# Two-layer graph attention, one core: the loop of the engines runs four groups in a turn in place of one

## The chip, the cores and the metric

The kernel runs on one core of one Trainium2 chip. The metric is the time of one execution on the device in microseconds (us), the median of three runs. Both kernels compute the same outputs.

## What is computed

128 graphs of 128 nodes with 384 features pass two residual blocks. Each block normalises the rows, applies a relu, projects to q, k and v with 384x384 weights, and attends with 12 heads of 32. The first block masks the scores where the adjacency is zero and adds 0.1 times the adjacency; the second adds the adjacency as a bias, treats rows that are all zero, and has an output projection.

```python
h = relu(layernorm(x))
q, k, v = heads(h @ W0q + b0q), heads(h @ W0k + b0k), heads(h @ W0v + b0v)
s = where(adj > 0, q @ k.T / sqrt(32) + beta * adj, -9e15)
x = x + join(softmax(s) @ v)
h = relu(layernorm(x))
q, k, v = heads(h @ W1q.T), heads(h @ W1k.T), heads(h @ W1v.T + b1v)
s = q @ k.T * 384 ** -0.5 + adj          # rows that are all 0 give 0
x = x + join(softmax(s) @ v) @ W1o.T + b1o
```

## The kernel before, in words

Four graphs make a group, so there are 32 groups. A unit is one layer of one group, 64 units in all, and the units are interleaved (`unit`, `loop_unit`, lines 83 to 94): layer 0 of the next group runs ahead of layer 1 of this one. A phase (`Phase`, line 97) is a slice of time in which several units are at different stages: the tail of one unit, the attention of the next, the projections of the one after it, the scores that are already looked up for that one, and the layer norm of a fourth. A phase has twelve slots (4 graphs by 3 chunks of four heads) with some places in each, and the constants of lines 39 to 73 say in which slot and place each step is issued.

Each engine has its own stream of instructions, written out by its own `phase` function, and `run_phases` (line 160) lays the phases out for it: the phases of `before()` written out one after the other, then a hardware loop (`Fori`, line 163) whose body holds the two phases of `inside(i)`, for i from 2 to 29, then the seven phases of `after()` written out. The first two phases of `after()` are the same phases as a turn of the loop. All five engines, SyncE (SP, which issues every DMA), GpSimd (POOL), ScalarE (ACT), VectorE (DVE) and TensorE (PE), run such a loop. They are tied together by semaphores alone: a wait compares a semaphore with a count that is worked out from the unit's number, `u.n`, which within the loop is a register expression of i.

The lines that the prediction speaks of:

- PE: projections L839 (`project`), scores L852, transposes of the probabilities L862, probabilities times values L879, output projection L913 to L917, and the transposes of the inverse sums L899 (`turn_inverse`), which wait for DVE's `inv_wide` L702.
- DVE: biased scores L647 behind a small memset L621 (`carry`) that carries waits, the inverse sums L689 to L702, and `take_v` L724, the last thing that a phase issues on DVE.
- ACT: exponentials L539, the copy of the turned probabilities L564, the high part of the output L578 (`high_o`), which PE's L913 waits for, and the first instructions that a turn issues on ACT.
- All: L163, the `Fori` itself, with its addition, its compare and branch, and the first register operation of a turn.

Of the kernel before, what the change touches and what calls it, by code (L numbers as in the profile page):

```python
# [90 lines left out]
def loop_unit(i, off):  # L91
    if off % 2:
        return Unit(i * 2 + off, 0, i + (off + 1) // 2, i + (off - 1) // 2, 1)
    return Unit(i * 2 + off, 1, i + (off // 2 - 1), i + off // 2, 0)
# [25 lines left out]


FIRST_LOOP, LAST_LOOP = 2, GROUPS - 3


def before():
    u = unit
    return [
        Phase(norm=u(0)),
        Phase(project=u(0), norm=u(1), look=u(0), bias=0),
        Phase(attend=u(0), project=u(1), look=u(1), bias=1),  # L130
        Phase(tail=u(0), norm=u(2)),
        Phase(attend=u(1), project=u(2), norm=u(3), look=u(2), bias=2, keep=0),
        Phase(attend=u(2), project=u(3), norm=u(4), look=u(3), tail=u(1)),
    ]


def inside(i):
    return [
        Phase(tail=loop_unit(i, -2), attend=loop_unit(i, -1), project=loop_unit(i, 0),
              look=loop_unit(i, 0), norm=loop_unit(i, 1), bias=i + 1, keep=i - 1),  # L140
        Phase(tail=loop_unit(i, -1), attend=loop_unit(i, 0), project=loop_unit(i, 1),
              look=loop_unit(i, 1), norm=loop_unit(i, 2)),
    ]


def after():
    u, n = unit, UNITS
    return [
        Phase(tail=u(n - 6), attend=u(n - 5), project=u(n - 4), look=u(n - 4), norm=u(n - 3),
              bias=GROUPS - 1, keep=GROUPS - 3),  # L150
        Phase(tail=u(n - 5), attend=u(n - 4), project=u(n - 3), look=u(n - 3), norm=u(n - 2)),
        Phase(tail=u(n - 4), attend=u(n - 3), project=u(n - 2), look=u(n - 2), keep=GROUPS - 2),
        Phase(tail=u(n - 3), norm=u(n - 1)),
        Phase(attend=u(n - 2), project=u(n - 1), look=u(n - 1)),
        Phase(tail=u(n - 2), attend=u(n - 1), keep=GROUPS - 1),
        Phase(tail=u(n - 1)),
    ]


def run_phases(eng, phase, first=0):  # L160
    for p in before()[first:]:
        phase(p)
    with eng.Fori(FIRST_LOOP, LAST_LOOP + 1) as i:  # L163
        for p in inside(i):
            phase(p)
    for p in after():
        phase(p)

# [37 lines left out]
def build(nc, x, adj, w0q, b0q, w0k, b0k, w0v, b0v, beta, w1q, w1k, w1v, b1v, w1o, b1o, out):  # L206
    weights = (w0q, w0k, w0v, w1q, w1k, w1v, w1o)
    w_scale = (QK0_SCALE, QK0_SCALE, W_SCALE, W_SCALE, W_SCALE, W_SCALE, W_SCALE)
    with ExitStack() as ctx:
# [143 lines left out]
        def _(sp):  # L353
# [30 lines left out]
            def phase(p):  # L384
                for s in range(SLOTS):
# [43 lines left out]
                    if s == 11 and p.look is not None and isinstance(p.look.n, int) and p.look.n == UNITS - 1:  # L429
                        sp.wait_ge(neg_ready, p.look.n * SLOTS)  # L430
                        sp.dma_start(adj1[:, :, :], adj_groups[p.look.group]).then_inc(adj1_in, 16)

            run_phases(sp, phase)
            for b in range(GROUP):
                sp.wait_ge(stored[b], 16 * GROUPS)

        @block.gpsimd
        def _(pool):
# [65 lines left out]
            def phase(p):  # L504
                for s in range(SLOTS):
# [14 lines left out]
                    if p.keep is not None and s in KEEP_SLOTS:  # L520
                        add_out_bias(p.keep, KEEP_SLOTS.index(s))

            run_phases(pool, phase)

        @block.scalar
        def _(act):
# [86 lines left out]
            high_weights(3, WEIGHTS)  # L613
            act.wait_ge(cols_ready, 3)
            run_phases(act, phase, 1)

        @block.vector
# [362 lines left out]
```

## Time and profile before

| | |
|---|---|
| median of 3 runs | 2375.24 us (2373.09 to 2375.53) |
| profiled execution | 2368.63 us |
| its span, first to last instruction | 2366.8 us |
| PE busy | 2208.3 us, 93% |
| ACT busy | 2058.5 us, 87% |
| DVE busy | 1834.5 us, 78% |
| POOL busy | 1521.9 us, 64% |
| DMA queue of the program | 66.4% of 16 engines |

The profile is of one execution. Busy shares are unions of instruction times; register, branch, semaphore and DMA-issuing instructions aren't counted as busy and are shown with a "q" behind the engine's name. "issue" as the releaser of a wait means that the engine waited for nothing that the profile shows. PEclk is the granted share of TensorE's clock: 1.00 is 2.4 GHz and 0.50 is 1.2 GHz. PEld is the weight load, which overlaps PE.

### The profile page before, as it was taken

The numbers are of one execution on the slowest core, as the hardware profiler recorded it, in microseconds if no ns is written. First come the engines' busy times: TensorE is split into PE (matmuls) and PEld (weight loads), VectorE is DVE, ScalarE is ACT, GpSimd is POOL, SyncE is SP. The second block draws the span as 40 slices with busy tenths as digits, with TensorE's granted clock in tenths as the row PEclk, the third lists the DMA queues.
The fourth block names the chain that finished last, engine by engine and source line by source line (L and its number), as shares of the span: only waits on it lengthen the run. The fifth ranks groups of instructions, "written<-read, shape, count | busy, mean of one in ns | idle before, by whom it ended". The sixth has DMA issues, their size and how long they took to land.

```text
span 2366.8 us, 77473 instructions
## 1 busy us (share of the span) xinstructions
PE 2208.3 (93%) x19968; PEld 1441.5 (61%) x19968; DVE 1834.5 (78%) x10186; ACT 2058.5 (87%) x7816; POOL 1521.9 (64%) x2439
## 2 busy tenths in 40 slices
PE   3699999999999999999999999999999999999977
PEld 1366666666666666666666666666666666666645
DVE  4478778787788887778788778787878787788856
ACT  3599998898898898898898898998998998899967
POOL 3276667676666676666676666676666676677645
PEclk9799999999999999999999999999999999999989
DMA  7587675686676676675776676776666776666731
GB/s 176 109 133 128 130 135 122 129 148 115 127 136 122 132 148 114 127 135 117 138 139 120 126 131 122 141 137 119 129 130 122 142 134 121 130 128 134 119 85 46
DMA packets 461103, 300.48 MB, mean 127 GB/s; under 512 B 228432, under 2 KB 460880, under 8 KB 460880
## 3 DMA queue, kind: packets, MB, share of 16 engines
q1 hardware_dynamic: 460880, 298.45, 66.4%
q14 instruction: 198, 1.62, 0.3%
q8 instruction: 25, 0.41, 0.1%
HBM read 71.83 MB, written 25.17 MB: 41 GB/s over the span
## 4 chain that ended last, share of the span: by engine, by line
PE 72%; DVE 14%; issue 8%; POOL 1%; DMA 1%; ACT 1%; DVEq 1%; SPq 1%; POOLq 0%; ACTq 0%
PE job_bank L839 43%; PE pt_bank L862 11%; PE score_bank L852 6%; PE o_bank L879 6%; DVE neg L647 4%; PE inv_bank L899 2%; PE post_bank L891 2%; DVE v L724 2%; DVE inv_wide L702 1%; DVE row_sum L691 1%; DVE live L697 1%; DVE off_zero L693 1%; DVE neg_max L647 1%; PE post_bank L917 1%; PE post_bank L913 1%
## 5 line engine op out<-in xcount | busy, mean ns | idle before, releaser
L539 ACT ACTIVATE probs<-neg,neg_max 128x128 f32<-128x128 f32 x3072 | 1189.7, 394 | 99.8 <-DVE neg_max L647 99.8
L839 PE MATMUL job_bank<-h,w_hi 128*128 128x512 f16 x2304 | 746.4, 391 | 73.9 <-DMA h<-h_rows 41.2
L539 ACT ACTIVATION_READ_ACCUMULATOR probs<-neg,neg_max 128x1 f32 x3072 | 595.4, 194 | 0.0
L564 ACT ACTIVATE probs_t<-pt_bank 128x512 f32<-128x512 f32 x768 | 450.5, 587 | 49.4 <-PE pt_bank L862 45.3
L862 PE MATMUL pt_bank<-ident,probs 128*128 128x128 f32 x3072 | 473.5, 278 | 9.4 <-ACT probs_t L564 8.4
L839 PE MATMUL job_bank<-h,w_lo 128*128 128x512 f16 x1152 | 448.7, 389 | 0.0
L862 PEld LDWEIGHTS pt_bank<-ident,probs 128*128 128x128 f32 x3072 | 375.5, 144 | 97.0 <-issue 17.8
L478 POOL TENSOR_TENSOR pair_sum<-neg 128x256 f32<-128x256 f32 x384 | 279.8, 729 | 217.8 <-DVE neg_max L647 207.9
L839 PE MATMUL job_bank<-w_hi,h 128*128 128x384 f16 x1536 | 413.5, 327 | 0.2 <-DVE part_lo L710 0.2
L839 PEld LDWEIGHTS job_bank<-h,w_hi 128*128 128x128 f16 x2304 | 224.7, 100 | 280.6 <-issue 91.8
L647 DVE CUSTOM_DVE_ANT_0 neg<-score_bank,bias 128x128 f32<-128x128 f32 x1536 | 353.6, 286 | 45.0 <-issue 42.5
L647 DVE CUSTOM_DVE_ANT_0 neg<-score_bank,adj 128x128 f32<-128x128 f32 x1536 | 353.4, 286 | 18.9 <-issue 18.9
L852 PEld LDWEIGHTS score_bank<-stack 96*128 96x128 f16 x3072 | 235.5, 98 | 130.0 <-issue 14.6
L852 PE MATMUL score_bank<-stack 96*128 96x128 f16 x3072 | 303.9, 222 | 3.5 <-DMA stack<-part_lo 2.7
L453 POOL TENSOR_TENSOR rstd<-shift_var,minus_half 128x1 f32<-128x1 f32 x256 | 140.7, 550 | 203.7 <-DVE shift_var L680 201.7
L647 DVE DVE_READ_ACCUMULATOR2_ANT neg_max<- 128x1 f32 x3072 | 254.4, 83 | 0.0
L469 POOL TENSOR_TENSOR h_rows<-h_rows 128x384 f16<-128x384 f32 x256 | 239.2, 934 | 21.4
L839 PE MATMUL job_bank<-w_lo,h 128*128 128x384 f16 x768 | 251.0, 327 | 0.0
L492 POOL TENSOR_TENSOR x_mid<-x_res,o_rows 128x384 f32<-128x384 f32 x128 | 127.9, 999 | 172.8 <-DVE o_rows L753 153.0
L879 PE MATMUL o_bank<-probs_t,v 128*32 128x128 f32 x6144 | 221.3, 277 | 1.4 <-ACT probs_t L564 1.4
L715 DVE SCALAR_TENSOR_TENSOR part_lo<-job_bank,part_hi 128x512 f16<-128x512 f32 x192 | 132.6, 691 | 108.4 <-ACT part_hi L555 107.8
L484 POOL TENSOR_TENSOR four_sum<-pair_sum 128x128 f32<-128x128 f32 x384 | 176.4, 459 | 31.0
(57 smaller groups left out, 3516.1 us busy)
## 6 DMA issues: line engine op xcount, KB each, us to landing
stack<-part_hi SPq DMA_DIRECT2D x768, 128.0 KB, 3.4
stack<-part_lo SPq DMA_DIRECT2D x384, 128.0 KB, 3.9
x_norm<-in_x SPq DMA_DIRECT2D x32, 768.0 KB, 6.2
x_res<-in_x SPq DMA_DIRECT2D x32, 768.0 KB, 5.1
out_x<-result SPq DMA_DIRECT2D x128, 192.0 KB, 3.3
adj<-in_adj SPq DMA_DIRECT2D x64, 256.0 KB, 3.1
h<-h_rows SPq DMA_TRANSPOSE x256, 3.9
stack<-in_L_gnn_Wq SPq DMA_DIRECT2D x2, 576.0 KB, 7.3
```

Source lines behind the costliest of these rows:

```text
L453: pool.tensor_tensor(rstd[:, b % 2:b % 2 + 1], shift_var[:, b % 2, 1:2], minus_half[:, :], ALU.pow).then_inc(rstd_done, 1)
L469: pool.tensor_tensor(h_rows[b % 2][:, 1, :], h_rows32[:, :], h_rows[b % 2][:, 0, :], ALU.subtract).then_inc(h_rows_ready, 1)
L478: pool.tensor_tensor(pair_sum[:, :, :], neg[c % 2][:, :, 0:NODES // 2], neg[c % 2][:, :, NODES // 2:NODES], ALU.add).then_inc(pair_sum_don ...
L484: pool.tensor_tensor(four_sum[b % 2][:, first:first + HC, :], pair_sum[:, :, 0:NODES // 4], pair_sum[:, :, NODES // 4:NODES // 2], ALU.add ...
L539: last = act.activation(probs[c % 2][:, h, :], neg[c % 2][:, h, :], ACT.Exp, bias=neg_max[:, b, first + h:first + h + 1], scale=-1.0, accu ...
L564: act.activation(probs_t[b % 2][:, first:first + HC, :].rearrange("p h q -> p (h q)"), pt_bank[:, :], ACT.Copy).then_inc(probs_t_ready, 1)
L647: last = dve.tensor_tensor_reduce(out=neg[c % 2][:, h, :], in0=score_bank[c % 2][:, P * h:P * (h + 1)], in1=bias, scale=(-1.0 / SCORE0 if ...
L715: last = dve.scalar_tensor_tensor(part_lo[t][:, c, :], job_bank[j % 2][:, :], scale, part_hi[t][:, c, :], ALU.mult, ALU.subtract)
L839: last = pe.matmul(to, stationary, moving, start=(m == 0), stop=(m == MATMULS - 1))
L852: last = pe.matmul(score_bank[c % 2][:, P * h:P * (h + 1)], q[0:3 * HEAD, c % KC, h, nodes], k[0:3 * HEAD, c % KC, h, nodes], start=True, ...
L862: last = pe.transpose(pt_bank[:, P * h:P * (h + 1)], probs[c % 2][:, h, :], ident[:, :])
L879: last = pe.matmul(o_bank[d:d + HEAD, f:f + P], v32[u.parity][:, b, HEAD * h:HEAD * (h + 1)], probs_t[b % 2][:, h, :], start=True, stop=True)
```

## The change

The loop takes steps of four, and its body holds the eight phases of `inside(i)` to `inside(i + 3)` one after the other. Its bounds become 2 and 27, so it has 7 turns in place of 28 and covers the same i from 2 to 29. The phases, the order of the instructions within them and the semaphores stay; the counts that the waits compare with are worked out from i + k in place of i. The code ahead of the loop and behind it stays.

```diff
 FIRST_LOOP, LAST_LOOP = 2, GROUPS - 3
+TURN = 4
...
 def run_phases(eng, phase, first=0):
     for p in before()[first:]:
         phase(p)
-    with eng.Fori(FIRST_LOOP, LAST_LOOP + 1) as i:
-        for p in inside(i):
-            phase(p)
+
+    with eng.Fori(FIRST_LOOP, LAST_LOOP + 2 - TURN, TURN) as i:
+        for k in range(TURN):
+            for p in inside(i + k):
+                phase(p)
     for p in after():
         phase(p)
```

## Rows read from the trace of the kernel before

**Rows 1.** The chain of work that ended last: start us, us, what.

```profile
251.00 2.48 issue
...
320.98 2.93 issue
...
2102.27 2.44 issue
```

**Rows 2.** Instructions of line 163 between 240 and 260 us, the first turn's end.

```profile
L163 SPq COMPARE_BRANCH  x1: 63/63/63, 243.6 to 243.6; - x1
L163 SPq FUSED_REGOPS  x1: 51/51/51, 243.9 to 243.9; - x1
L163 PEldq COMPARE_BRANCH  x1: 247/247/247, 248.3 to 248.3; - x1
L163 PEldq FUSED_REGOPS  x1: 59/59/59, 248.6 to 248.6; - x1
L163 ACTq COMPARE_BRANCH  x1: 45/45/45, 249.9 to 249.9; - x1
L163 ACTq FUSED_REGOPS  x1: 65/65/65, 250.2 to 250.2; - x1
L163 DVEq COMPARE_BRANCH  x1: 68/68/68, 250.4 to 250.4; - x1
L163 DVEq FUSED_REGOPS  x1: 85/85/85, 253.5 to 253.5; - x1
```

**Rows 3.** Waits of PE, DVE and ACT from 251.00 to 2172.21 us: total, times, longest.

```profile
PE inv_bank L899 <- DVE inv_wide L702: 59.7, 27, 2.6
...
DVE carrier_v L621 <- issue: 78.8, 27, 3.3
...
ACT probs L539 <- DVE neg_max L647: 89.4, 81, 2.3
```

**Rows 4.** Windows: start:end length, busy us (count) of each engine, PEclk, DMA share, GB/s.

```profile
2172.21:2239.55 67.34, 67.04 (x626) 44.49 (x625) 56.34 (x321) 63.50 (x245) 47.58 (x76) 1.00 0.72 123
183.59:251.00 67.41, 67.25 (x626) 44.23 (x625) 56.80 (x319) 63.75 (x246) 47.50 (x76) 1.00 0.74 139
392.74:464.25 71.51, 69.06 (x626) 45.22 (x625) 56.94 (x319) 64.11 (x245) 47.49 (x76) 0.98 0.69 129
678.80:748.58 69.78, 67.63 (x626) 44.32 (x626) 56.78 (x319) 63.87 (x245) 47.49 (x76) 1.00 0.70 132
251.00:2172.21 1921.21, 1856.71 (x16849) 1214.92 (x16848) 1536.99 (x8588) 1729.08 (x6589) 1282.55 (x2052) 0.98 0.69 130
```

**Rows 5.** A stretch of 3.4 us some 7 us behind a turn's start, same columns.

```profile
471.30:474.70 3.40, 3.40 (x15) 2.04 (x14) 2.80 (x18) 2.58 (x10) 2.35 (x5) 0.50 0.00 0
```

**Rows 6.** DMA queues from 251.00 to 2172.21 us: packets, MB, share of 16 engines.

```profile
q14 instruction: 161, 1.32, 0.3%
```

**Rows 7.** DMA queues from 2172.21 to 2239.55 us, same columns.

```profile
q8 instruction: 5, 0.08, 0.6%
q14 instruction: 8, 0.07, 0.4%
```

**Rows 8.** Timeline around the first turn's end: DVE, ACT and PE in turn.

```profile
249.98 1.01 DVE L724 SCALAR_TENSOR_TENSOR v<-job_bank,bv_rows 128x384 f32<-128x384 f32 x2
253.81 0.06 DVE L621 MEMSET carrier_v<- 128x1 f32 x1 [2.81 <-issue]
...
250.47 0.51 ACT L578 ACTIVATE o_hi<-o_norm 128x384 f16<-128x384 f32 x1
...
254.82 0.40 ACT L539 ACTIVATE probs<-neg,neg_max 128x128 f32<-128x128 f32 x1 [1.82 <-DVE neg_max L647]
...
251.93 0.32 PE L913 MATMUL post_bank<-w_hi,o_hi 128*128 128x384 f16 x1
...
253.92 0.86 PE L879 MATMUL o_bank<-probs_t,v 128*32 128x128 f32 x24
256.90 0.55 PE L899 MATMUL inv_bank<-ident,inv_wide 128*128 128x128 f32 x3 [2.11 <-DVE inv_wide L702]
```

## The prediction

> **What bounds the kernel now.** I read the chain of waits first. It runs through PE's matmuls nearly everywhere, and once in each turn of the loop it has a piece called "issue", of 2.4 to 2.9 us, in which nothing that the profile shows was waited for [rows 1]. The pieces begin exactly where DVE's last `take_v` of a turn ends, so they sit on the loop's back edge. The instructions of the loop's own line say what happens there. SP, PE, ACT and POOL go from their compare-and-branch to the first register operation of the next turn in some 0.3 us; DVE takes 3.1 us (250.4 to 253.5) [rows 2]. So DVE's sequencer is without instructions for about 3 us at each of the 27 taken back edges. The waits confirm it: DVE's carrier stood idle 78.8 us in 27 pieces for "issue", and PE waited 59.7 us in 27 pieces, 2.21 us each, for DVE's `inv_wide` [rows 3]. PE is the bound and passes each of these waits on.
>
> The windows tell what a turn costs with and without the edge. The last two phases written out ahead of the loop and the first two behind it do the work of a turn with no taken branch in between: 67.41 and 67.34 us, with PE busy 67.25 and 67.04 us of it at clock 1.00. The loop's turn at 392.74 us took 71.51 us at a mean clock of 0.98, that at 678.80 us 69.78 us at 1.00, and all 27 together 1921.21 us, 71.16 each [rows 4]. So the mean back edge costs 71.16 - 67.38 = 3.78 us: 2.2 us of PE's wait, and some 1.5 us because in most turns the granted clock goes to 0.50 (1.2 GHz) for 3.4 us once PE has been idle [rows 5]. The turn without that drop cost 2.4 us, those with it some 4.1.
>
> **Fetching.** The loop moved 161 packets on the queue named instruction, q14, and none on q8; the written-out stretch behind it moved both [rows 6, 7]. 161 packets in 27 turns are six a turn. I read this as DVE fetching its body anew each turn, and stalling on the first packet alone, while PE's 1251 matmuls and loads in a turn (626 and 625) stay on the chip. ACT issues 245 counted instructions a turn and does not stall, DVE 319 and does [rows 2, 4]; the limit of what these two keep lies between, control instructions aside.
>
> The Trainium skill, page "Runtime: NRT & Kernel Launch", section Instruction fetch mechanics, says the same in figures: 512 instructions kept for most engines and 2048 for PE, and a stall where a taken branch leaves the window that is held. That four-fold bodies of ACT and PE miss would follow from it; no run here shows PE missing. The trace agrees in that DVE misses and PE doesn't, though DVE's 319 counted instructions alone would fit.
>
> **The change, part by part.**
>
> *21 back edges go.* Seven turns have 6 taken edges, in place of 27. At 3.78 us each, 21 give 79.4 us. What is late next in their place: nothing much, as the two written-out stretches show, where PE is busy 99.6% of the time and ACT 63.5 us of 67.3 [rows 4]. ACT is the next bound at about 94%, POOL and DVE have 20 and 11 us to spare.
>
> *Code in one piece costs more fetching.* The body now streams through PE's store too. The written-out stretch has just this: 5 packets on q8 and 8 on q14 in 67 us, and it ran at 67.34 us, so I price streaming at nothing, covered by the sequencers' lead over their engines [rows 4, 7]. If that cover failed, each missed packet would cost up to DVE's 3 us.
>
> *Waits with i + k.* The register operations in front of the waits may get one more addition. They run on the sequencers, which are ahead. The loop's turn at full clock took 69.78 us, and 69.78 less PE's wait of 2.2 is 67.6, against 67.38 with constant counts [rows 3, 4]: at most 0.2 us a group for register operations altogether. One more of them: between 0 and 0.2 us a group, 0 to 6 us in 28 groups; I take nothing, and keep 6 for the range.
>
> *The six edges left get dearer.* ACT's body grows to 980 counted instructions, POOL's to 304, PE's to some 5000, SP's likewise four-fold. ACT passes the size at which DVE misses by far, so ACT misses with DVE; PE, POOL and SP perhaps. The bounds: nothing more than now (3.8 us), if all misses lie beside DVE's; and one more 3.1 us after another for ACT and PE, with a second clock drop of 1.7, so 3.8 + 3.1 + 3.1 + 1.7 = 11.7 us. What the first turn's end says [rows 8]: ACT branches at 249.9 [rows 2] and would go on at 253.0. Its `o_hi`, now at 250.47, would come at 253.3 and end at 253.8. PE, which now starts L913 at 251.93, would wait 1.9 us there, then has the 2.85 us of work that now ends at 254.78, so is ready at 256.65, before `inv_wide` releases L899 at 256.90. Behind that, ACT's four exponentials (1.6 us) come after `o_hi` in place of before DVE's stall, so the copy L564 and with it PE's L879 come near 256.5, and L899 at about 257.3: 0.4 us more. ACT's next exponentials start at 256.4 rather than 254.82, 1.6 us late on an engine with 6% to spare. So between 0.4 and 1.6 us more, I take 1.2: 5.0 us an edge. PE's own miss would start at its branch, 248.3, 2.1 us ahead of DVE's; if it is as long as DVE's it ends at 251.4, before the place of L913 (251.93), and what it delays falls inside the wait that PE has there anyway. POOL has nothing to do behind its branch, and SP branches 7 us ahead of DVE with only loads due far later.
>
> **Sum.** Against the profiled execution of 2368.63 us (span 2366.8): 27 edges at 3.78 go, -102.1; 6 at 5.0 come, +30.0; net -72.1, so 2296.5 us. The median of the runs lies 6.6 us above the profiled execution; carried over, 2303 us.
>
> **The rivals.**
>
> *A. The misses add up at the six edges, or straight code is a little slower than the two stretches promise.* Five engines ask for code within 8 us, and each restart is followed by waiting for the next engine's. At 11.7 us an edge that is 6 x 6.7 = 40 us more: 2343. For it: ACT has little slack, and two stretches of 67 us are a thin base for 28 groups. Against: the misses start within 2.2 us of each other, so they overlap. A slip of 1 us a group in the long body would also give 28 us, 2331.
>
> *B. The six edges stay as cheap as now, or cheaper,* because PE's idle time doesn't always bring the half clock: at 2.4 to 3.8 us each, 7 to 16 us less than forecast, 2287 to 2296. For it: all stalls lie side by side by the working above.
>
> *C. Slower: the long body's fetching isn't hidden.* The place is each engine's crossing into code that isn't on the chip, now that PE, ACT and POOL stream as well as DVE. DVE's 3.1 us is the price. A turn of four groups has some 8 x 4 = 32 packets on q14 and 20 on q8 by the written-out stretch. The gain to be eaten is 72 us, 10.3 a turn; from four exposed misses a turn beyond the edge it is gone. With eight, 7 x 24.8 = 174 us more, 2477. Against it: DVE crosses into fetched code some five times a turn already and stalls once, and the stretches at both ends show none.
>
> *D. DVE's 3 us isn't fetching but a fixed price of something else in the loop's head,* so that it returns every two phases. The first phases behind the loop show no such stall [rows 4], so this has almost nothing; it would give 2375.
>
> **How the numbers follow.** Forecast, 5 us an edge and covered streaming: 0.62. A: 0.14. B: 0.17. C: 0.05. D: 0.02. The predicted time is the forecast's, 2303. The range goes from B's 2290 to where A is half in, 2328 (an edge of about 9 us, or 0.9 us a group); C, D and the rest of A are left out. 0.2%, 5 us, is about what a measurement of this kernel can tell from no change. Faster by more takes the forecast, A, B and a mild C: 0.95. Same: D, 0.02. Slower: C, 0.03.
>
> **What would show it.** In the new profile, "issue" waits of DVE's carrier should fall from 27 pieces to 6; the instructions of line 163 should show 6 taken branches with 3 us behind them on DVE and now on ACT, probably PE; a stretch of two phases inside a turn should be 67.4 us at clock 1.00, and a stretch over an edge about 72.4. PE's wait for `inv_wide` should fall from 59.7 to some 13 us, with a new wait for `o_hi` at the six edges. q8 should carry packets throughout. Wrong would be: pieces of "issue" in mid-turn (C), edges over 8 us or inner stretches over 68.4 (A), and no change of the turn per group (D).

## The result and the profile after

The changed kernel takes 2288.47 us in the median (2288.0 to 2290.1, 4 runs), against 2375.39 us for the kernel before, run beside it: a ratio of 0.9637, interval 0.9620 to 0.9653. It is faster by 87 us. The forecast was 2303 with a range from 2290 to 2328, so the direction and the cause hold and the gain was put too small: the time lies 1.5 us under the range. The profiled execution took 2290.10 us, its span 2288.3.

The windows of the kernel after, columns as in [rows 4]: the two phases written out behind the loop, three groups within the first turn, the group over the first taken edge, the one over the fourth, and the whole of the same 27 groups.

```profile
2093.98:2161.36 67.38, 67.21 (x627) 44.50 (x626) 56.65 (x320) 63.55 (x246) 47.49 (x76) 1.00 0.72 123
249.86:317.61 67.75, 67.11 (x626) 44.46 (x625) 56.59 (x321) 63.56 (x245) 47.61 (x76) 1.00 0.65 138
317.61:384.97 67.36, 67.16 (x626) 44.41 (x625) 56.90 (x321) 63.61 (x246) 47.49 (x76) 1.00 0.68 138
384.97:452.32 67.35, 66.78 (x623) 44.07 (x621) 56.90 (x319) 63.26 (x244) 47.48 (x76) 1.00 0.81 131
452.32:522.53 70.21, 68.18 (x627) 44.50 (x628) 56.78 (x321) 64.30 (x246) 47.43 (x76) 1.00 0.73 142
1271.35:1344.35 73.00, 69.71 (x626) 45.40 (x627) 56.95 (x320) 64.53 (x246) 47.44 (x76) 0.98 0.68 136
249.86:2093.98 1844.12, 1819.09 (x16850) 1198.35 (x16849) 1533.51 (x8587) 1719.49 (x6589) 1282.89 (x2052) 1.00 0.72 137
```

The 27 groups went from 1921.21 us [rows 4] to 1844.12. Within a turn a group takes what the written-out phases take, 67.4 us, with PE busy nearly throughout; the second group of each turn takes 67.75 to 67.84. (A turn's first group is the one over the edge, so the 67.75 us from 249.86 on are the second group of the first turn.) Only the groups over a back edge stand out, and there are six: 70.21, 70.90, 70.47, 73.00, 70.87 and 71.13 us, 426.58 together. The 21 others take the remaining 1417.54, 67.50 each, so an edge costs 3.60 us more than an inner group.

The loop's own line at the first turn's end (L165 now; the change put three lines in front of the rest), to be read against [rows 2]:

```profile
L165 SPq COMPARE_BRANCH  x1: 63/63/63, 444.9 to 444.9; - x1
L165 PEldq COMPARE_BRANCH  x1: 3928/3928/3928, 449.6 to 449.6; - x1
L165 SPq FUSED_REGOPS  x1: 51/51/51, 450.1 to 450.1; - x1
L165 ACTq COMPARE_BRANCH  x1: 45/45/45, 451.3 to 451.3; - x1
L165 DVEq COMPARE_BRANCH  x1: 68/68/68, 451.9 to 451.9; - x1
L165 PEldq FUSED_REGOPS  x1: 63/63/63, 453.6 to 453.6; - x1
L165 ACTq FUSED_REGOPS  x1: 59/59/59, 454.2 to 454.2; - x1
L165 POOLq COMPARE_BRANCH  x1: 45/45/45, 455.0 to 455.0; - x1
L165 DVEq FUSED_REGOPS  x1: 85/85/85, 455.1 to 455.1; - x1
L165 POOLq FUSED_REGOPS  x1: 68/68/68, 458.6 to 458.6; - x1
```

Now all five stall: SP for 5.2 us, PE for 4.0 (its branch itself lasts that long), ACT 2.9, DVE 3.2, POOL 3.6. Before, only DVE did. The waits over the 27 groups, and the queues (packets, MB, share), tell the same:

```profile
ACT o_hi L581 <- issue: 15.9, 6, 3.4
...
DVE carrier_v L624 <- issue: 11.4, 3, 4.0
...
PE inv_bank L902 <- DVE inv_wide L705: 10.1, 24, 1.7
PE job_bank L842 <- issue: 10.1, 6, 2.0
...
PE post_bank L916 <- ACT o_hi L581: 1.1, 2, 0.9
```
```profile
q8 instruction: 154, 2.52, 0.6%
q14 instruction: 264, 2.16, 0.5%
```

PE's wait for `inv_wide` fell from 59.7 us [rows 3] to 10.1, and in its place PE has six idle pieces of its own, 1.7 us each, in which it waits for nothing that the profile shows while its branch lasts 3.4 to 3.9 us. The new wait for `o_hi` that the prediction put at all six edges came at two, 1.1 us together. q8 now carries 154 packets where it had none; within these groups it has them only in the kernels in which TensorE's body is longer than one group, so they are TensorE's code, and TensorE pays for fetching it only at the six edges.

### The profile page after: what moved, and what is told of

It is laid out like the page before. It is cut to its first block, busy times and chain, and to the rows that moved or that the text cites. A ratio compares the mean times of both kernels' runs of the same rounds, so it can differ in the third digit from the quotient of the medians.

```text
span 2288.3 us, 76836 instructions
## 1 busy us (share of the span) xinstructions
PE 2170.5 (95%) x19968; PEld 1424.5 (62%) x19968; DVE 1831.0 (80%) x10186; ACT 2048.9 (90%) x7816; POOL 1522.4 (67%) x2439
## 4 chain that ended last, share of the span: by engine, by line
PE 85%; DVE 7%; issue 3%; POOL 1%; ACT 1%; DMA 1%; SPq 1%; DVEq 0%; ACTq 0%; POOLq 0%
PE job_bank L842 47%; PE pt_bank L865 13%; PE o_bank L882 7%; PE score_bank L855 7%; PE inv_bank L902 3%; PE post_bank L894 2%; PE post_bank L916 2%; PE post_bank L920 2%; PE post_bank L917 2%; DVE neg L650 2%; DVE inv_wide L705 1%; DVE part_lo L713 1%; ACT probs L542 1%; DVE row_sum L694 1%; DVE off_zero L696 1%
## 5 line engine op out<-in xcount | busy, mean ns | idle before, releaser
L842 PE MATMUL job_bank<-h,w_hi 128*128 128x512 f16 x2304 | 728.7, 382 | 81.7 <-DMA h<-h_rows 41.8
L865 PE MATMUL pt_bank<-ident,probs 128*128 128x128 f32 x3072 | 465.2, 274 | 11.4 <-ACT probs_t L567 10.4
L842 PE MATMUL job_bank<-h,w_lo 128*128 128x512 f16 x1152 | 439.7, 382 | 0.0
L865 PEld LDWEIGHTS pt_bank<-ident,probs 128*128 128x128 f32 x3072 | 366.6, 141 | 95.8 <-issue 13.5
L718 DVE SCALAR_TENSOR_TENSOR part_lo<-job_bank,part_hi 128x512 f16<-128x512 f32 x192 | 132.6, 691 | 107.3 <-ACT part_hi L558 105.3
```

The source lines that it names most:

```text
L718: last = dve.scalar_tensor_tensor(part_lo[t][:, c, :], job_bank[j % 2][:, :], scale, part_hi[t][:, c, :], ALU.mult, ALU.subtract)
L842: last = pe.matmul(to, stationary, moving, start=(m == 0), stop=(m == MATMULS - 1))
L865: last = pe.transpose(pt_bank[:, P * h:P * (h + 1)], probs[c % 2][:, h, :], ident[:, :])
```

## The experiments

In all of them `turn` is the number of groups in a turn, given engine by engine, and 28 means no loop: the groups from 2 to 29 written out one after the other with constant counts. All leave the work and its order alone.

```diff
-def run_phases(eng, phase, first=0):
+def run_phases(eng, phase, first=0, turn=1):
...
+    if turn == LAST_LOOP + 1 - FIRST_LOOP:
+        for i in range(FIRST_LOOP, LAST_LOOP + 1):
+            for p in inside(i):
+                phase(p)
+    else:
+        with eng.Fori(FIRST_LOOP, LAST_LOOP + 2 - turn, turn) as i:
+            for k in range(turn):
+                for p in inside(i + k):
+                    phase(p)
```

The experiments ran on three chips, each beside the kernel before, which takes 2368 to 2369 us in the median on every one of them, so their times are compared with each other to about 1 us and the ratios stand beside them. Beside the changed kernel the kernel before took 2375.39 us, so for the changed kernel the ratio is the safer number. In the experiments' kernels line 169 is the loop's own, and the lines behind it stand seven further down than in the kernel before.

### Whose loop is it? VectorE alone at four groups, and all but VectorE

```diff
-            run_phases(dve, phase, 1)
+            run_phases(dve, phase, 1, turn=4)
```

> Only VectorE's loop holds four groups in a turn; the other four engines keep the loop of one group. Theory (the back edge costs what VectorE's fetching of its body costs, and nothing else): 21 of 27 stalls go and the other engines don't stall at all, so the time is that of the change, 2288 us, give or take 4. Rival 1 (part of the gain came from the other engines' longer bodies, which take fewer turns too): the time stays well above 2288, near 2330. Rival 2 (at the six edges left the other engines' own stalls make them dearer): up to 8 us below 2288. PE's waits for inv_wide: 6 long ones of 2.2 us.

> The reverse: SP, GpSimd, ScalarE and TensorE hold four groups in a turn, VectorE keeps the loop of one. Theory: VectorE's 27 stalls stay, and at 6 edges the others stall beside it: 2375 us, 2370 to 2385. Rival (the turns of the other engines cost as well): near 2330. With it comes the price of TensorE's and ScalarE's stalls where VectorE stalls anyway: the six edges that both have against the 21 that VectorE has alone.

VectorE alone: 2286.23 us, ratio 0.9657 (0.9640 to 0.9674). All but VectorE (VectorE's `turn` 1, the default 4): 2366.71 us, ratio 0.9995 (0.9981 to 1.0009). The whole gain of the change comes with VectorE's body alone, and without VectorE's there is no gain that can be told from none; rival 1 is out. The second time lies under the span expected, 2370 to 2385, because that was reckoned from 2375 and the kernel before took 2367.75 here. The waits over the 27 groups of the kernel with VectorE alone at four, and its windows over the first and the fourth edge:

```profile
PE inv_bank L906 <- DVE inv_wide L709: 18.6, 27, 2.0
DVE carrier_v L628 <- issue: 10.6, 4, 2.7
DVE carrier_v L628 <- ACT probs L546: 5.2, 2, 2.6
```
```profile
452.80:522.66 69.86, 67.60 (x628) 44.31 (x625) 56.81 (x319) 63.98 (x245) 47.60 (x76) 1.00 0.68 131
1271.50:1342.60 71.10, 68.98 (x626) 45.10 (x624) 58.38 (x329) 64.16 (x245) 47.60 (x76) 0.98 0.68 130
```

Over its inner groups of 67.5 its edges cost 2.4 us where the clock stays at 1.00 and 3.6 where it falls; before it was 2.4 and 4.1 [rows 4]. In the changed kernel the five edges without the fall cost 3.2 on the mean over 67.50 (70.72). So the other engines' stalls do add, 0.8 us by these profiles. In the kernel of all but VectorE the two kinds of stall were laid over each other at 6 of 27 edges, and the median moved by 1 us, within the interval.

### No edges at all

```diff
-            run_phases(dve, phase, 1)
+            run_phases(dve, phase, 1, turn=28)
```

> VectorE's 28 groups written out with no loop, the other engines keep the loop of one group. Theory: no stall is left, so all 27 edges of 3.8 to 4.1 us go: 2375 - 27 x 4 = 2267 us (2264 to 2274), and the pace is 67.4 us a group throughout, granted clock 1.00 in the whole stretch. Rival (the branches of the other engines cost something of their own, or VectorE's long stream of code does): 2280 or more.

> All five engines written out, no loop at all and all waits against constants. Theory: as with VectorE alone written out, 2267 us, the streaming of TensorE's code being hidden; with no register operations perhaps 3 us less. Rival (streaming TensorE's and ScalarE's code costs something that the loop of one group did not pay): slower than VectorE alone written out, by 0.1 to 0.5 us a group, 3 to 14 us.

VectorE alone written out: 2261.14 us, ratio 0.9550 (0.9533 to 0.9568), the fastest kernel of the study, and 3 us under the span expected, which again started from 2375. All five written out: 2262.49 us, ratio 0.9558 (0.9540 to 0.9575). VectorE alone written out, then all five, over the 27 groups:

```profile
250.44:2066.10 1815.66, 1810.25 (x16850) 1198.60 (x16849) 1530.93 (x8589) 1717.32 (x6590) 1282.43 (x2052) 1.00 0.74 137
```
```profile
250.76:2067.13 1816.37, 1809.91 (x16850) 1200.21 (x16849) 1518.36 (x8588) 1716.61 (x6590) 1284.43 (x2052) 1.00 0.77 138
```

1815.66 / 27 is 67.25 us a group, with PE busy 99.7% of it: nothing but PE's own work is left on the path. PE streams all its code in the second kernel and loops over one group in the first, and they differ by 0.7 us in 1816. Streaming in a straight line costs nothing that can be measured, so rival C of the prediction had no ground. The loops of one group that SP, POOL, ACT and PE still run in the faster kernel, 27 taken branches each, are free as well.

The instruction queue q14 over the 27 groups of VectorE alone written out, against 161 packets with its loop of one group [rows 6]:

```profile
q14 instruction: 81, 0.66, 0.1%
```

The other engines' code is the same in both, so the loop fetched twice as many packets as the same work written out.

### Is it the fetching? Telling the branch's target ahead

```diff
-        with eng.Fori(FIRST_LOOP, LAST_LOOP + 2 - turn, turn) as i:
+        with eng.bass.Fori(FIRST_LOOP, LAST_LOOP + 2 - turn, turn, engines=[eng.engine], hint_back_edge=hint) as i:
```

This puts one instruction at the head of each turn that names the closing branch, for VectorE alone in the kernel of one group, and for all five in the changed kernel.

> The kernel before, one group in a turn on all engines, with one thing added: VectorE's loop tells at the head of each turn where its closing branch goes, so that the target's code can be fetched ahead. Theory (the 3 us are the fetch of the code at the branch's target): VectorE's stall goes without any unrolling, 27 edges fall from 3.5 to 4 us to some 0.3, and the time is near the 2261 us of VectorE written out, 2261 to 2275; extra packets on q14. Rival (a taken branch on a body of this size costs 3 us whatever is fetched, or the long body helps in another way): 2360 or more.

> The changed kernel, four groups in a turn on all engines, with the same telling ahead on all five. Theory: the six edges lose the stalls of all engines, 6 x 3.6 = 22 us, 2262 to 2270 us. Rival (with five engines missing, or with bodies this long, the fetch ahead is overwritten before the branch comes): 2288, no change.

One group, VectorE's told ahead: 2311.97 us, ratio 0.9760 (0.9744 to 0.9776). The unrolling isn't needed for the larger part of the change's gain, so fetching the target has a part in the stall; but a part stays, and the time lies outside both spans expected. Line 169 there, at one edge:

```profile
L169 DVEq COMPARE_BRANCH  x1: 68/68/68, 387.5 to 387.5; - x1
...
L169 DVEq BRANCH_PREFETCH_HINT  x1: 39/39/39, 389.5 to 389.5; - x1
```

DVE goes on after 2.0 us instead of 3.1 [rows 2], not after 0.3 as expected. PE's waits for `inv_wide` are 1.2 us each (31.6 in 27), and the granted clock never fell in the 27 groups: an edge costs 1.7 us (1865.74 / 27 is 69.10, less 67.4). Where the clock held, an edge cost 2.4 us before, so the shorter stall itself is worth 0.7 us an edge, 19 us; the larger part of the saving of 56 us is the clock's, which no longer falls. Why 2 us are left, and whether they too are fetching, isn't settled.

Four groups, all told ahead: 2290.11 us, ratio 0.9662 (0.9646 to 0.9678), no gain over the change. PE's branch fell from some 3.5 us to 0.9 in the median and SP's next turn began 0.3 us after the branch in place of 5.2, but DVE still stood:

```profile
L169 PEldq COMPARE_BRANCH  x7: 88/925/1568, 450.3 to 2091.6; - x7
```
```profile
DVE carrier_v L628 <- issue: 20.0, 6, 3.9
```

6 pieces, 3.3 us each. From its branch to its next turn VectorE took 2.8 to 3.6 us; that was 3.2 to 4.7 in the changed kernel, where all five engines stall, and 2.8 with VectorE alone at four groups. PE's own pause is gone, and in its place PE waits 2.4 to 3.2 us for `inv_wide` at each edge; the clock fell at four of the six. So the rival was right about the time, and VectorE's stall alone sets the price. Whether the fetch ahead was overwritten on the way is only argued.

### The number of edges

> Seven groups in a turn on all engines: 4 turns, 3 taken edges. Theory (time = 2262 us + 3.6 to 4 us for each taken edge): 2273 us, 2270 to 2277. Rival (something grows with the length of the body): 2280 or more.

> Two groups in a turn on all engines: 14 turns, 13 taken edges. Theory (2262 us + 3.6 to 4.4 us for each taken edge, since the bodies of TensorE with some 2500 and ScalarE with some 490 counted instructions now stall too): 2310 us, 2306 to 2320. Rival (the edges are cheaper where the other engines' bodies still fit): 2295 to 2304.

With `turn` at 7 and at 2 on all engines: 2276.93 us (ratio 0.9618, 0.9598 to 0.9637) and 2315.91 us (ratio 0.9784, 0.9767 to 0.9800). Both lie in the theory's span. From no edge (2262.49), 3 edges cost 14.4 us and 13 cost 53.4: 4.8 and 4.1 each. With the kernel before, 27 edges cost 105.3, 3.9 each. Not all of the 4.8 is the edges': in the profiles the inner groups of these two kernels take 67.42 and 67.46 us, against 67.27 with everything written out, and over that their edges cost 3.6 and 3.7 us. The time goes by the number of taken edges and a little for the loop's inner groups; no growth of an edge with the length of the body shows.

### What each engine's stall costs by itself

With VectorE written out, the six edges of four groups were given to the other four engines, to TensorE alone, to ScalarE alone, and to TensorE and SP.

```diff
-            run_phases(pe, phase, 2)
+            run_phases(pe, phase, 2, turn=4)
```

> VectorE written out with no loop, the other four engines with four groups in a turn: the six edges hold the stalls of TensorE, ScalarE, GpSimd and SP without VectorE's. Theory (the stalls lie side by side, so each engine's own of about 3 us costs TensorE some 2 us, whoever else stalls): 2261 + 6 x 2 to 3 = 2273 to 2279 us, near what VectorE's stalls alone cost (2286 - 2261 = 25 us for six) and no less than half of it. Rival (the stalls of the other four are covered by the lead of their sequencers and only VectorE's counts): 2261 to 2265.

> Only TensorE has a loop body that outgrows its store (four groups in a turn); VectorE is written out, SP, GpSimd and ScalarE keep one group in a turn. Theory: TensorE's pause of 1.5 to 2.0 us at its own fetch, six times, with no or few drops of the clock: 2261 + 9 to 15 = 2270 to 2276. Rival (its matmuls queued ahead cover the fetch): 2263 or less.

> Only ScalarE has a body of four groups; VectorE is written out, SP, GpSimd and TensorE keep one group in a turn. My working of the prediction: o_hi comes 2.9 us late, TensorE waits 1.9 us for it before its output projection, at six edges: 2261 + 6 x 1.9 = 2272 (2269 to 2276). Rival (ScalarE's lateness is taken up by work that TensorE has in hand): 2261 to 2265.

| at four groups | time, us | over 2261.14, for each edge |
|---|---|---|
| ScalarE | 2274.24 | 2.2 |
| TensorE | 2288.46 | 4.6 |
| TensorE and SP | 2273.95 | 2.1 |
| TensorE, ScalarE, GpSimd, SP | 2279.30 | 3.0 |

(Ratios 0.9602, 0.9664, 0.9599 and 0.9618, intervals within 0.0018 of each.) For all four the time expected was 2273 to 2279. ScalarE's case came close to the prediction's working, in price more than in kind: an edge took 2.0 us more than an inner group, of which 1.2 us are PE's wait for `o_hi`, where the working had 1.9, and some 0.5 a wait for the turned probabilities. Its timeline and PE's at one edge, ACT's branch being at 450.7:

```profile
453.26 0.52 ACT L585 ACTIVATE o_hi<-o_norm 128x384 f16<-128x384 f32 x1 [1.97 <-issue]
```
```profile
453.84 0.34 PE L920 MATMUL post_bank<-w_hi,o_hi 128*128 128x384 f16 x1 [1.18 <-ACT o_hi L585]
```

TensorE alone was the surprise: 12 us over the span expected, and dearer than all four together. The window over the first edge took 70.42 us without a fall of the clock, against 69.56 for the four; and at the other five the clock fell, against three of six. Its branch lasted longer, and SP went on as ever behind its own, so that a load of `adj` went out at 448.22 us, just before TensorE's branch at 448.5, and another load and a store within it. Hence the last run:

> As the run with TensorE's body alone at four groups (2288.5 us), but SP has four groups in a turn too; VectorE written out, GpSimd and ScalarE with one group. There TensorE's branch took 4.2 to 5.1 us, with SP's loads of adj and its store issued at the same moment; with all four engines at four groups it took 3.9 to 4.0 and the time was 2279.3. Theory (TensorE's fetch waits behind the transfers that SP has just issued; where SP stalls too, from about 444 to 450 us, the queues are empty when TensorE asks): the branch takes 3.9 to 4.0 us and the time is 2275 to 2281. Rival (it is something that ScalarE's or GpSimd's stall spares): 2286 to 2291 as with TensorE alone.

2273.95 us: 14.5 us less than TensorE alone, by giving SP a stall too. PE's branch at the first edge, TensorE alone and then with SP:

```profile
L169 PEldq COMPARE_BRANCH  x1: 4948/4948/4948, 448.5 to 448.5; - x1
```
```profile
L169 PEldq COMPARE_BRANCH  x1: 3468/3468/3468, 448.2 to 448.2; - x1
```

Over the six edges it lasted 4.2 to 5.1 us alone and 3.5 to 4.1 with SP, and the clock fell at five edges against one. The time came 1 us under the theory's span and far from the rival's. That TensorE's branch lasts longer where SP doesn't stall, and so issues a transfer just before it, is what these two runs show; that the fetch waits behind the packets is the reading that fits, and no run separates it from other effects of SP's timing.

## Why the prediction was right and where it was wrong

*The bound and the cause* hold. DVE's back edge, and no other engine's, cost 3.8 us on the mean in the 27 turns; the two single-sided kernels show it. That the stall is fetching is borne out by the told-ahead branch for some 1 us of its 3.1, and by the packets that fall from 161 to 81. The price of 102 us for all 27 is what VectorE written out gives: its 27 groups take 1815.66 us, 105.6 less than before, of which 3.5 is the inner pace of 67.25 in place of 67.38.

*Code in one piece costs nothing more* holds, by the kernels with no edges.

*Waits with i + k* were taken at nothing, with 6 us kept, and that holds: the third and fourth groups of a turn, whose waits have i + 2 and i + 3, took 67.36 us, as much as the written-out phases. But the inner groups took 67.50 on the mean, 3.2 us more than 67.38 over 27 groups, and nearly all of it is the second group of each turn. There DVE stands still once, ahead of `live`, and PE's wait for `inv_wide` is 0.64 us in place of 0.20; DVE's piece is in all seven second groups and in no other of the 27, and neither in the kernel before nor with VectorE written out:

```profile
305.06 0.19 DVE L700 SCALAR_TENSOR_TENSOR live<-row_sum,off_zero 128x12 f32<-128x12 f32 x1 [0.49 <-DVE off_zero L696]
```
```profile
305.97 0.55 PE L902 MATMUL inv_bank<-ident,inv_wide 128*128 128x128 f32 x3 [0.64 <-DVE inv_wide L705]
```

So it hangs on one place in the long body. What it is stays open.

*The six edges left get dearer* was the step that was mis-sized: 5.0 us predicted, 3.60 measured, 8.4 us over the six. The base was wrong. The 3.8 us of an edge before hold a fall of the clock in 22 of 27 cases, worth some 1.5 us, and I let it stand for all six. After the change the clock fell at one edge of six. Why it holds there isn't shown: PE's own idle piece at an edge is 1.5 to 2.0 us in place of 2.2 for `inv_wide`, but with VectorE alone at four groups, with pieces of 2.0, it fell at three of six, and with two groups in a turn and pieces up to 2.9 at eight of thirteen, not always at the longest.

The part added for the other engines, 1.2 us taken and 0.7 to 0.8 measured where the clock held, came near by luck, for its working failed. It had ACT's late `o_hi` hold PE up for 1.9 us and PE's own miss cost nothing, because a miss of 3.1 us would end before L913's place. What came is the reverse: PE's branch lasted 3.4 to 3.9 us and PE ran out of work within it, standing 1.7 us on the mean at each edge, and behind that it waited for `o_hi` at two edges only. At the first edge PE's idle piece began at 451.95 us, 2.3 us after the branch, so even 3.1 us would not have been covered. What does hold is that PE is idle while DVE is, so that only what is left over adds.

*The sum against the profiled execution* was 2296.5 us; it came to 2290.1. To within rounding the 6.4 us are the edges' 8.4, less 3.2 for the inner groups, plus 1.4 outside the 27 groups.

*The step to the median* failed by more than that. I carried over the 6.6 us by which the median before lay above its profiled execution. After the change the median lies 1.6 us below it: 8.2 us of the 14.6 by which the forecast was too high. A difference between two executions isn't a price of the work, and nothing in the rows bore it out. Where it comes from stays open. On one chip 13 runs of the kernel before spread from 2362.42 to 2373.19 us, and by their mean granted clocks, 0.975 to 0.977 in the four fastest and 0.972 to 0.975 in the four slowest, that spread goes with how often the clock fell; the kernel with VectorE written out, in which it never fell in the 27 groups, spreads by 2.1 us in four runs. But chance falls of the clock don't explain why the profiled execution was quick: its own mean clock is 0.972, as low as any of those runs has. Its 2368.63 us are what the kernel before takes on the experiments' chips, 2368 to 2369, and it is the median of 2375 that stands apart, which might be the chip; no run separates the two.

*The rivals.* B was nearest, with the six edges as cheap as before; its span, 2287 to 2296 with the same offset, holds the measured time, and the range was cut 3 us above its lower end. But by its own sum edges of 3.60 us give 2294.6; that the time came near its foot is the offset's doing. A, C and D are out, but for one trace of C, the half microsecond in mid-turn told above, if that is fetching.

## What to carry to other kernels

Look for an "issue" piece at the head of each turn of a hardware loop, and compare a turn with the same phases written out behind the loop: that difference times the taken edges is what a longer body or no loop gives. The engine to unroll is the one that stands still behind its branch; here VectorE alone written out brought 0.955, as much as all five written out, 0.956, and VectorE alone at four groups as much as all five at four, and it left the others' code small. And a stall on the path costs more where the clock falls behind it, 4.1 us in place of 2.4 here; that second part came at 22 edges of 27 in one kernel and at one of six in another, so it should be priced apart from the stall and not carried over with it.

## What the runs showed of the hardware that I had not expected

How long a body may be before its engine stalls at the taken branch shows across these traces, counting every instruction from one branch to the next, register, wait and branch instructions included. ScalarE at 350, GpSimd at 320 and SP at 212 went on after some 0.3 us; SP at 416, VectorE at 474, GpSimd at 634 and ScalarE at 697 stalled. TensorE at 1360 went on and at 2717 stalled.

Telling the branch's target ahead took TensorE's branch from some 3.5 to 0.9 us and SP's stall from 5.2 to 0.3, but VectorE's only from 3.1 to 2.0 with one group, and with four it left 2.8 to 3.6. And stalls of two engines can be cheaper than one: TensorE and SP together cost 12.8 us over six edges, TensorE alone 27.3.
